# Fused RNN, FFN and routed-expert kernel: one register load for all table values, a place for every tile's rows, and the second layer's biases laid into the second output as one product

## What is computed

```python
logits = x_flat @ gate_w.T
probs = softmax(logits)
topk_probs, topk_idx = top_k(probs, 2)
hidden = relu(einsum('th,ehf->tef', x_flat, w1) + b1)
all_out = einsum('tef,efh->teh', hidden, w2) + b2
y = sum(all_out at topk_idx * topk_probs)
return x + y
```

## Time and profile before

| what | us |
|---|---|
| median of 3 runs | 519.46 (518.76 to 521.85) |
| the profiled execution | 516.84 |
| its span | 514.8 |
| from the span's start to the first result added (start of GpSimd's first DMA of L742) | 398.57 |
| from there to the start of its last tile's first DMA | 100.51 |
| from there to the end of the span | 15.7 |

### The profile page before, as it was taken

One profiled execution on the slowest core, in us unless ns is written; L12 is line 12 of the kernel. 1 busy time (PEld: TensorE's weight loads), 2 busy tenths in 40 slices (PEclk: granted clock), 3 DMA queues, 4 the chain that ended last, 5 costly groups with the idle time before them and its releaser, 6 DMA issues.

```text
span 514.8 us, 9104 instructions
## 1 busy us (share of the span) xinstructions
PE 437.1 (85%) x2391; PEld 367.1 (71%) x2391; DVE 403.0 (78%) x932; ACT 351.8 (68%) x766; POOL 205.0 (40%) x196
## 2 busy tenths in 40 slices
PE   8998999999999998999889899997019888888840
PEld 7984787777777776887767688886009787788830
DVE  2576699999999999998976999889817675667621
ACT  2335688889988888998888687985018675677710
POOL 3125343342244555230002206336600775676780
PEclk9996799999999999999989999999557998899985
DMA  3883344448544444453997112001350436676616
GB/s 101 224 217 117 140 164 163 163 173 282 218 163 169 173 187 180 188 225 123 355 361 218 46 55 84 18 28 40 110 159 1 54 72 150 130 177 173 124 18 228
DMA packets 49366, 76.85 MB, mean 149 GB/s; under 512 B 8949, under 2 KB 36278, under 8 KB 45494
## 3 DMA queue, kind: packets, MB, share of 16 engines
q1 hardware_dynamic: 36454, 59.84, 34.9%
q10 hardware_dynamic: 5232, 12.27, 6.4%
q0 software_dynamic: 7648, 4.36, 6.1%
HBM read 50.69 MB, written 18.77 MB: 135 GB/s over the span
## 4 chain that ended last, share of the span: by engine, by line
DVE 31%; PE 27%; issue 17%; DMA 14%; ACT 4%; POOL 3%; DVEq 3%; SPq 1%; ACTq 1%; POOLq 0%
DVE hid_lo L1068 10%; PE ps L1359 5%; PE ps L1360 5%; PE ps L1361 5%; DVE hid_lo L1157 4%; DVE yg L1062 4%; DMA out_d<-ysb,xrow 3%; DMA xrow<-disp 3%; DMA rawf<-in_L_ffn_w_dram 2%; DMA out_dram<-xtok 2%; PE ps L1637 2%; DVEq L1294 2%; POOL out_dram L742 2%; PE ps L1429 2%; DMA out_dram<-ysb,xrow 1%
## 5 line engine op out<-in xcount | busy, mean ns | idle before, releaser
L1068 DVE TENSOR_TENSOR hid_lo<-yg,hid_hi 128x512 fp32r<-128x512 f32 x124 | 97.2, 784 | 0.0
L797 ACT ACTIVATE hid<-ps,bias_cur 128x512 f32<-128x512 f32 x128 | 86.5, 676 | 11.4 <-PE ps L1361 10.6
L818 ACT ACTIVATE hid_hi<-yg 128x512 fp32r<-128x512 f32 x124 | 77.8, 628 | 20.5 <-DVE yg L1062 19.6
L630 POOL TENSOR_TENSOR w2l<-raw,w2h 128x128 fp32r<-128x128 f32 x32 | 25.3, 791 | 108.7 <-ACT w2h L767 108.7
L853 ACT ACTIVATE hid<-ps,cols 128x512 f32<-128x512 f32 (+3 forms) x84 | 52.8, 629 | 18.5 <-PE ps L1361 12.7
L1359 PE MATMUL ps<-in_hi,w1h 128*128 128x512 f32 x128 | 53.8, 420 | 6.3 <-POOL w1l L630 5.8
L742 POOL DMA_INDIRECT out_dram<-ysb,xrow x24 | 39.5, 1644 | 43.5 <-DVE ysb L1343 37.9
L1157 DVE TENSOR_TENSOR hid_lo<-hid,hid_hi 128x512 fp32r<-128x512 f32 (+3 forms) x84 | 50.5, 624 | 7.6 <-ACT hid_hi L857 6.5
L703 POOL DMA_INDIRECT disp<-stage,idx x32 | 34.0, 1062 | 50.3 <-issue 30.2
L1062 DVE TENSOR_TENSOR yg<-hid,h_f 128x512 f32<-128x512 f32 x60 | 50.6, 844 | 1.6 <-DMA h_f<-gt_d 1.0
L1361 PE MATMUL ps<-in_hi,w1l 128*128 128x512 f32 x128 | 51.3, 401 | 0.0
(11 more groups left out here) (232 smaller groups left out, 1209.0 us busy)
## 6 DMA issues: line engine op xcount, KB each, us to landing
gb<-gt_d SPq DMA_DIRECT2D x15, 1024.0 KB, 4.6
h_f<-gt_d SPq DMA_DIRECT2D x14, 1024.0 KB, 4.5
disp<-empty ACTq DMA_DIRECT2D x16, 616.5 KB, 6.8
w1d<-wf SPq DMA_DIRECT2D x15, 512.0 KB
rawf<-in_L_ffn_w_dram SPq DMA_DIRECT2D x16, 256.0 KB, 2.9
xrow<-disp SPq DMA_DIRECT2D x23, 137.0 KB, 2.5
raw<-in_L_ffn_We_dram SPq DMA_DIRECT2D x2, 960.0 KB, 8.4
nat<-in_x_dram SPq DMA_DIRECT2D x8, 128.0 KB, 3.1
```

The source lines that it names most:

```text
L797: nc.scalar.activation(hid0[:, m % 4, :], bank(4 + m % 4), ACT.Gelu, bias=bias0_cur[:, e_par:e_par + 1]).then_inc(s_hid0, 1)
L818: nc.scalar.activation(hid_hi0[:, m % 8, :], src[:, m % 4, :], ACT.Copy).then_inc(s_hi0, 1)
L1068: V.tensor_tensor(hid_lo0[:, m % 8, :], src[:, m % 4, :], hid_hi0[:, m % 8, :].bitcast(F32), ALU.subtract).then_inc(s_lo0, 1)
```

## The change

1. The three engines that need numbers of `tab` read each list with one `values_load_multi_w_load_instructions`. It stands for one TENSOR_LOAD, and the two register instructions for each of the 15 values remain (rows ISA x30 below). SyncE reads both lists ahead of the first `weights`.
2. Each of the 23 tiles has its own place for its rows, in `xrow_a` (16 tiles) and `xrow_b` (7), and its own semaphore. `load` waits for nothing any more, and in SyncE's list all loads stand ahead of `weights` from tile 10 on.
3. `b2s`, `b2raw` and the biases' product in `out_of` (L1632) go. Instead GpSimd fills `b2diag` (128 x 2048) with zeros, and SyncE lays `fb2` (8 x 128) 16 times on its diagonal. After the routing ScalarE makes the exponentials of all tokens, VectorE the gates of all experts (`gates_of_tokens`), TensorE transposes them and multiplies them with `b2diag` in four products of 512 columns, ScalarE copies these to `obias`, and SyncE writes that to `out2` in 8 DMAs. The zero fill of `out2` goes, and tile 1's add waits for those writes.

```diff
@@ sync
+            sp.wait_ge(s_b2z, 1)
+            for i in range(TILES):
+                sp.dma_start(b2diag[i * EF:(i + 1) * EF, i, :], fb2).then_inc(s_b2, 16)
             for k in range(WR, 2 * EF):
...
             def load(t):
-                dst = xrow[:, t % XR, :, :]
-                if t >= XR:
-                    added(sp, t - XR)
...
+            for t in range(STATIC):
+                load(t)
+            for k in range(4):
+                sp.wait_ge(s_ob, k + 1)
+                for s in range(2):
+                    sp.dma_start(out2_v[s, :, 4 * k:4 * k + 4, :],
+                                 obias[64 * s:64 * s + 64, 4 * k:4 * k + 4, :]).then_inc(s_base2, 16)
             sp.wait_ge(s_tab, 2)
+            _, first_of = nc.values_load_multi_w_load_instructions(
+                tab[0:1, 0, 0:DYN], engines=[mybir.EngineType.SP], min_val=0, max_val=(RANKS - TS) * S1 + EF)
...
-            for t in range(XR, NTAU):
+            for t in range(STATIC, NTAU):
                 load(t)
-                if STATIC + 2 <= t - 1:
-                    weights(t - 1)
-            weights(NTAU - 1)
+            for t in range(STATIC + 2, NTAU):
+                weights(t)
@@ gpsimd
             def biases():
-                pool.wait_ge(s_b2, 16)
                 pool.wait_ge(s_agg, 3)
-                link(G.tensor_scalar(b2raw[:], b2raw[:], ident[:, 0:1], None, ALU.mult))
-                link(G.tensor_copy(b2s[:, :, 0, :], b2raw[:]))
-                G.tensor_tensor(b2s[:, :, 1, :], b2raw[:], b2s[:, :, 0, :].bitcast(F32),
-                                ALU.subtract).then_inc(s_b2s, 1)
+                pool.wait_ge(s_xtp, Q1)
+                G.memset(b2diag[:], 0.0).then_inc(s_b2z, 1)
...
+                if t == 1:
+                    pool.wait_ge(s_base2, 16 * 8)
@@ scalar
+            act.wait_ge(s_row, NG)
+            A.activation(gat[:], stage[:, :, D + 1:ROW], ACT.Exp).then_inc(s_gexp, 1)
+            for k in range(4):
+                act.wait_ge(s_obp, k + 1)
+                A.activation(obias[:, 4 * k:4 * k + 4, :].rearrange("p i d -> p (i d)"), bank(4 + k),
+                             ACT.Copy).then_inc(s_ob, 1)
@@ vector
+            def gates_of_tokens():
+                dve.wait_ge(s_gexp, 1)
+                link(V.tensor_reduce(gsum[:], gat[:], AX, ALU.add))
+                link(V.reciprocal(grec[:], gsum[:]))
+                link(V.tensor_tensor(gat[:], gat[:], taken_f[:], ALU.mult))
+                V.tensor_tensor(gat[:], gat[:], grec[:].unsqueeze(2).broadcast_to([P, TILES, EF]),
+                                ALU.mult).then_inc(s_gat, 1)
+                dve.wait_ge(s_gatp, 1)
+                V.tensor_copy(gatT[:], ps[:, 2, 128:256]).then_inc(s_gatT, 1)
...
             route1_places(NG - 1)
+            gates_of_tokens()
             tables()
@@ tensor
+            M.transpose(ps[:, 2, 128:256], gat[:].rearrange("p i e -> p (i e)"), ident[:]).then_inc(s_gatp, 1)
+            pe.wait_ge(s_b2, 16 * TILES)
+            pe.wait_ge(s_gatT, 1)
+            for k in range(4):
+                M.matmul(bank(4 + k), gatT[:], b2diag[:, 4 * k:4 * k + 4, :].rearrange("p i d -> p (i d)"),
+                         start=True, stop=True).then_inc(s_obp, 1)
...
-                    M.matmul(o[:, 0:2 * P], ones_r[:], b2s[:, e, :, :].rearrange("p o a b -> p (o a b)"),
-                             start=True, stop=False, skip_group_check=True)
```

More of the change, by code:

```diff
@@ L143, in build @@
         x_f = at("x_f", 0, [P, NT], F32)
-        xrow = at("xrow", 8 * KB, [P, XR, 2, ROW], F32)
+        xrow_a = at("xrow_a", 96 * KB, [P, XR, 2, ROW], F32)
+        xrow_b = at("xrow_b", 8 * KB, [P, NTAU - XR, 2, ROW], F32)
         h_f = at("h_f", 8 * KB, [P, NT], F32)
@@ L295, in build @@
         s_disp = sem("s_disp")
-        s_ld = [sem(f"s_ld{k}") for k in range(XR)]
+        s_ld = [sem(f"s_ld{k}") for k in range(NTAU)]
         s_w1d = [sem(f"s_w1d{k}") for k in range(2)]
@@ L372, in build @@
         s_wfl = sem("s_wfl")
-        s_b2s = sem("s_b2s")
+        s_b2z = sem("s_b2z")
+        s_gexp = sem("s_gexp")
+        s_gat = sem("s_gat")
+        s_gatp = sem("s_gatp")
+        s_gatT = sem("s_gatT")
+        s_obp = sem("s_obp")
+        s_ob = sem("s_ob")
         s_lgf = sem("s_lgf")
@@ L418, in added, with xrow @@
             eng.wait_ge(s_sa[t % 2], 32 * (t // 2 + 1))
+        def xrow(t):
+            return xrow_a[:, t, :, :] if t < XR else xrow_b[:, t - XR, :, :]
         def merge(eng, parts):
@@ L549, in load @@
             def load(t):
-                dst = xrow[:, t % XR, :, :]
-                if t >= XR:
-                    added(sp, t - XR)
[L554 to L560, removed]
+                rows_of = disp_rs[0:TS, t, :] if t < STATIC else disp[bass.ds(first_of[t - STATIC], TS, step=S1), :]
+                sp.dma_start(xrow(t), rows_of.rearrange("(a p) c -> p a c", p=P)).then_inc(s_ld[t], 16)
             def weights(t):
                 j = t - STATIC
-                e = sp.value_load(tab[0:1, 1, j:j + 1], min_val=0, max_val=EF - 1)
+                e = expert_of[j]
                 if j >= 2:
@@ L1293, in _ @@
             dve.wait_ge(s_tab, 2)
-            expert_of = [dve.value_load(tab[0:1, 1, j:j + 1], min_val=0, max_val=EF - 1) for j in range(DYN)]
+            _, expert_of = nc.values_load_multi_w_load_instructions(
+                tab[0:1, 1, 0:DYN], engines=[mybir.EngineType.DVE], min_val=0, max_val=EF - 1)
             def split_x(t):
@@ L1600, in turn @@
                 for a in range(2):
-                    op = M.transpose(bank(t % 2)[:, a * P:(a + 1) * P], xrow[:, t % XR, a, 0:D], ident[:])
+                    op = M.transpose(bank(t % 2)[:, a * P:(a + 1) * P], xrow(t)[:, a, 0:D], ident[:])
                 op.then_inc(s_tr, 1)
@@ L1641, in out_of @@
                     op.then_inc(s_m2, 1)
-            pe.wait_ge(s_b2s, 1)
+            pe.wait_ge(s_ob, 4)
             pe.wait_ge(s_tab, 2)
-            expert_of = [pe.value_load(tab[0:1, 1, j:j + 1], min_val=0, max_val=EF - 1) for j in range(DYN)]
+            _, expert_of = nc.values_load_multi_w_load_instructions(
+                tab[0:1, 1, 0:DYN], engines=[mybir.EngineType.PE], min_val=0, max_val=EF - 1)
             for t in range(2):
```

53 lines of the change are left out of this document (25 added, 28 removed).

## The result

The changed kernel takes 503.38 us (median of 4 runs, 502.20 to 503.89), against 519.71 for the kernel before beside it: a ratio of 0.968 (0.964 to 0.971), 16.3 us faster. The forecast was 500.7 in a range of 495 to 511. The profiled execution took 503.57, its span 501.8; that is 13.0 less than the span of before, where the steps summed to 18.8. Four runs of before beside e1 to e4 (518.47, 521.14, 726.2 and 1085.09 us) and one of e11 (622.56 us, at a mean granted clock of 0.64) were slow ones and are in no ratio.

What follows compares the result with a forecast made beforehand. No engine was full: a VectorE gap ahead of tile 0 and tiles waiting for each other in a ring were taken as the bound. Terms -3.9 - 13.0 - 1.9 = -18.8 us gave 498.0 profiled, 500.7 median, range 495 to 511.

Steps and rivals of the forecast that it cites:

- Register loads: VectorE ahead of tile 0: one bulk load of 0.3 us cuts the gap from 10.34 to about 4.5, 5.8 less.
- R1: Rival: the bulk register load pays by value, so 14 x 0.30 = 4.2 us comes back, 504.9; chance 0.12.
- Gates of tokens: Way into the FFN: five VectorE instructions ahead of the tables and hand-overs to TensorE add 1.9 us.
- GpSimd's biases: Near 280 us: GpSimd's work on the biases goes, and TensorE's wait of 1.88 with it, 1.9 us less.
- The 16 small loads: SyncE, ahead of rawf piece 3: 5.5 us of issues, piece 3 lands at 279.6, nothing gained or lost.
- R3: Rival: SyncE's 16 small loads meet a full queue at 271 us, slower by 8, 527; chance 0.03.
- The pace: FFN tiles: with a place for every tile, 22 steps take 87.5 in place of 100.5 us, 13.0 less.
- step (c): Dynamic tiles: weights of tile t need tile t-2's last relu, 4.03 us a tile, taken as 4.05.
- R2: Rival: copies and adds slow each other, tiles stay near 4.5 us, 513.7 to 515; chance 0.09.
- The product in the tiles: TensorE's biases' product, 0.35 us a tile, costed at nothing; up to 8 us if TensorE decided.
- Covers: What is late next: TensorE ready near 377 against VectorE near 381; SyncE's weights at 395, writes by 385.
- The offset: Profiled execution forecast at 498.0; the median shown was 2.6 above the profile, so 500.7 for the median.

Runs made afterwards that it cites:

- e1: The kernel before with the bulk register loads alone, on VectorE, TensorE and SyncE: ratio 0.985 (0.978 to 0.992).
- e4: The kernel after with VectorE reading its 15 expert numbers singly, two behind each of tiles 0 to 7: ratio 0.967 (0.960 to 0.975).
- e11: The kernel after with three weight places, VectorE's single reads in tiles 3 to 7, TensorE's bulk load ahead of its wait for ScalarE's copies: 0.952.
- e9: The kernel before, unchanged, profiled on the same chip as the kernel after: 521.53 us in 8 runs, ratio 1.001.
- e10: The kernel after, unchanged, profiled on the same chip as the kernel before: 501.99 us in 2 runs, ratio 0.964.
- e8: The kernel before with GpSimd's last instruction on the biases replaced by a zero fill: 515.45 us in one run, before beside it 519.38.
- e6: The kernel after with three places for the copied first-layer weights and their biases: 499.77 us, ratio 0.965.
- e3: The kernel before with the biases' part alone, ring of 7 places and single register loads kept: ratio 0.997 (0.992 to 1.001).
- e2: The kernel before with a place for every tile's rows and all loads ahead of the weights from tile 10 on: ratio 0.978.
- e5: The kernel after, unchanged, run and profiled once more: 501.21 us, ratio 0.967 (0.962 to 0.972).

## Why the prediction was right, and where its terms were off

The direction, the places and the order of the terms were right; the forecast missed the median by 2.7 us. That it came so near is in part luck, as the last two points say. Term by term, with the pair of one chip (e9, e10):

- *Register loads*, predicted -5.8: -4.6 (the gap 10.33 to 5.71, in e1 too). The step that failed is "one load of 0.3 us (in the worst case 0.9)": it took 1.80, while the register work came cheaper, 0.30 a value and not 0.32. R1 said that the load pays by value. By my estimate it pays some 0.1 us a value (1.4 to 2.0 for 15, against 0.30 for one), a third of R1's price, so truth lay between forecast and rival.
- *Gates of tokens*, predicted +1.9: +2.0.
- *GpSimd's biases*, predicted -1.9: 2.4 in e8 (68.7 to 66.3), 3.1 in e10 with the rest of the part. The term was too small because the row I priced (3.35 for 1.29) was not all: the wait for piece 3 fell by 0.9 and the cast beside GpSimd's work by 0.3. *The 16 small loads* were priced rightly to the tenth (5.5, measured 5.39), and in after piece 3 landed a good microsecond earlier than the 279.6 I gave. The range's lower end, 495, counted on the memset's luck as well. No run shows that term: in none of the eight profiles with the memset does a cast of VectorE run beside it. The memset took 1.81 and held a copy for up to 1.0 us, of which no later stretch shows anything. R3 is out: 0.34 an issue where it needed 1.55.
- *The pace*, predicted -13.0 with 87.5 for 22 steps: 89.8, 86.2 and 85.9 in three profiles of after, -10.7 to -15.6. The step (c) that gave the dynamic tiles 4.05 described a wait that is there but decides little (e6): tiles 7 to 22 are 3.88 apart in e10. GpSimd's DMAs and the tiles that fill the pipeline decide. What I had not seen is TensorE's clock. A wait of 2.29 us was followed by 5 us at a granted clock of 0.66 and a step of 6.94, which is most of the difference between 89.8 and 85.9. And such falls (0.59 and 0.57) stood behind long waits of the old ring as well, 2.10 and 2.43 us: of the 100.5 that I took for the price of waiting, 3.8 are missing in e8, where the clock stayed up. Both are argued from the rows, since no run took only the clock away; e1 and e3, with three falls each, take 98.7 and 97.5. By e8 against e10 the places alone are worth 10.8, less than my 13.0. R2 is out.
- *The product in the tiles*, predicted 0: 0.4 to 0.7 (86.6 in e2 against 86.2 and 85.9 in e5 and e10), less than after's own profiles differ by.
- *Covers*: TensorE was ready at 379.3, not 377, since its bulk load cost 6 and not 5 us and stood behind the copies; still 4 ahead of VectorE, whose reads end at 383.5. SyncE's first weights left at 394.3 (said: 395), the writes by 383.2 (said: 385). Both covered (398 less 385 would have been 13 us, not the 10 that I gave).
- *The offset* between profile and median was the weak step, and here the luck lies. For a profiled execution I forecast 498.0, and it took 503.57; only the 2.6 added for the median brought the forecast near. The profile of after lies 0.2 above its median, so the 2.6 was no offset of this kernel. That it came from halts of ScalarE in the other runs of before fits e9 (a profile with halts, 0.25 above its median), but is not shown, as those runs have no trace; in e3 a profile without halts is 3.6 below the median, in e1 1.5 above it.
- *The sum.* In one chip's profiles my sum, 18.8, meets 19.1. Of that 2.7 were lost again in a later start of the layer. This start differs by up to 5.3 us between the profiles, 4.5 of them already there at the end of the 31-expert layer, near 240 us, ahead of what the change moves. So the sum agreed better than its terms did.

The three parts alone give 1.5, 2.2 and 0.3% (e1 to e3), together 4.0, where after gives 3.2 to 3.6; within the intervals they add up.

## What to carry to other kernels

When a ring's wait is taken away, price the two rings behind it as well: here the dynamic tiles stood at 3.88 us and GpSimd alone needs 3.72, so the next edit (a third place) brought about 1 us, within the noise, and not 4. Instructions that can wait until they are needed (register reads for tile 8) belong neither ahead of tile 0 nor among the tiles that fill the pipeline, and a load for registers belongs ahead of a wait it doesn't need. Before spans of two profiles are subtracted, compare a stretch that the change did not touch, and the granted clock in the stretch that it did: here the clock stood at 0.66 over the 5 us behind a wait of 2.29 us, and the kernel before had two such falls in its tiles.

## What the runs showed of the hardware that was not expected

- A bulk register load of 15 values from SBUF takes 1.38 to 1.97 us on VectorE, TensorE and SyncE in after; a single one takes 0.30 in before.
- ScalarE stands still for 1.8 to 1.9 us, in after with its input ready, at the same instruction of the 5-expert layer, in every profile of two chips (e5 to e11) and in none of a third (e1 to e4); 4.5 to 4.9 us are lost by unit 20. The granted clock is 1.00 from 300 to 355 us in either kind. The cause is open; no run tried to move it.
- TensorE's granted clock fell after an idle 2.29 us in the tiles and stood at 0.66 over the next 5 us. The length of one idle time does not say it: the clock fell behind 1.76 us (e9) and stayed at 1.00 behind 2.11 (e3), 2.15 (e4) and 2.36 (e9).
- Beside a memset of GpSimd (1.81 us) a VectorE copy of two elements a row takes 0.31 to 1.20 us in place of 0.16 and ends 0.02 to 0.03 behind the memset, in all eight profiles that have it, while VectorE's two-input instructions keep their 0.16 to 0.17.
